# Rounding the attention heads to fp8 on VectorE: five bf16 operations in SBUF in place of four through a PSUM bank

## What is computed

```python
FP8_MAX = 448.0
def _fp8_roundtrip(x):
    return x.astype(jnp.float8_e4m3fn).astype(jnp.float32)

def _div_clamp_fp8(x, scale):
    y = jnp.clip(x.astype(jnp.float32) / scale, -FP8_MAX, FP8_MAX)
    y = y.astype(jnp.bfloat16).astype(jnp.float32)
    return _fp8_roundtrip(y)
...
core = _gqa(q, k, v).reshape(b, s, nh * d)
xout = _gqa(qx, kx, vx).reshape(b, s, nh * d)
cat = jnp.concatenate([core, xout], axis=-1)
catq = _div_clamp_fp8(cat, proj_smooth)
return jnp.einsum('bsi,oi->bso', catq, wproj) * (proj_in_scale * proj_w_scale)
```

## Time and profile before

| | us |
|---|---|
| median of 3 runs | 1740.62 (1740.0 to 1741.47) |
| the profiled execution | 1740.71 |
| its span | 1738.9 |
| PE busy | 1648.4 (95%) |
| DVE busy | 1411.2 (81%) |
| ACT busy | 1357.8 (78%) |
| POOL busy | 1085.3 (62%) |

### The profile page before, as it was taken

The page is one execution under the profiler, slowest core; times in us unless marked ns, Lnnn a source line. Parts: engine busy times, 40 slices in busy tenths (PEclk is TensorE's granted clock), DMA queues, the critical chain, the costliest instruction groups (busy, mean ns, idle before and its releaser), DMA issues.

```text
span 1738.9 us, 44071 instructions
## 1 busy us (share of the span) xinstructions
PE 1648.4 (95%) x15776; PEld 1228.6 (71%) x15776; DVE 1411.2 (81%) x3223; ACT 1357.8 (78%) x2907; POOL 1085.3 (62%) x1031
## 2 busy tenths in 40 slices
PE   1459999999999999999999999999999999999999
PEld 1438788888888888888888888888888544444444
DVE  8999899999999999999999999998779762323232
ACT  6879999999999999999999999999999622122221
POOL 1347787778777777777777777777777613121211
PEclk9879999999999999999999999999999999999999
DMA  5937788887878888888788888877999980303000
GB/s 177 214 95 133 142 157 146 146 154 148 144 149 154 153 147 152 144 148 148 150 145 151 148 158 149 144 142 132 175 203 196 201 244 26 134 12 140 6 24 25
DMA packets 663555, 241.45 MB, mean 139 GB/s; under 512 B 619440, under 2 KB 635952, under 8 KB 662832
## 3 DMA queue, kind: packets, MB, share of 16 engines
q1 hardware_dynamic: 662048, 230.20, 67.2%
q0 software_dynamic: 1296, 8.52, 2.4%
HBM read 75.15 MB, written 29.51 MB: 60 GB/s over the span
## 4 chain that ended last, share of the span: by engine, by line
PE 80%; ACT 6%; DVE 5%; issue 3%; SPq 2%; POOL 2%; DMA 1%; ACTq 0%; POOLq 0%; DVEq 0%
PE ps_pj L662 25%; PE ps_o L709 6%; PE ps_o L711 6%; PE ps_o L710 6%; PE ps_s L725 5%; PE ps_s L726 5%; PE ps_s L729 5%; PE ps_s L669 4%; PE ps_qt L681 4%; PE ps_pj L798 2%; PE ps_s L813 2%; PE ps_o L799 2%; PE ps_pj L799 2%; PE ps_o L798 2%; PE ps_s L812 2%
## 5 line engine op out<-in xcount | busy, mean ns | idle before, releaser
L1092 POOL TENSOR_TENSOR local<-local 128x512 bf16<-128x512 f32 x512 | 593.3, 1159 | 289.2 <-ACT local L998 288.9
L662 PE MATMUL ps_pj<-wide 128*128 128x256 bf16 (+1 forms) x5544 | 584.0, 254 | 5.3 <-DVE wide L1172 4.5
L662 PEld LDWEIGHTS ps_pj<-wide 128*128 128x128 bf16 x5544 | 469.9, 98 | 116.4 <-DVE wide L1172 4.7
L995 ACT ACTIVATE local<-ps_s,neg_max 128x512 f32<-128x512 f32 x512 | 389.2, 760 | 35.9 <-DVE neg_max L1359 33.8
L998 ACT ACTIVATE local<-ps_s,neg_max 128x512 bf16<-128x512 f32 x512 | 391.4, 764 | 0.0
L709 PE MATMUL ps_o<-v_hi,local 128*128 128x129 bf16 x2048 | 375.9, 222 | 2.8 <-DMA local<-local 1.4
L711 PE MATMUL ps_o<-v_hi,local 128*128 128x129 bf16 x2048 | 375.5, 219 | 0.0
L710 PE MATMUL ps_o<-local 128*128 128x128 bf16 x2048 | 375.3, 218 | 0.0
L1359 DVE TENSOR_REDUCE neg_max<-ps_s 128x1 f32<-128x512 f32 x512 | 345.2, 674 | 22.7 <-PE ps_s L729 22.1
L926 ACT ACTIVATE local<-ps_pj,head_rstd 128x128 f32<-128x128 f32 x756 | 239.6, 439 | 42.9 <-issue 41.2
L1069 POOL TENSOR_TENSOR head_rstd<-sq_sum,minus_half 128x3 f32<-128x3 f32 x256 | 226.2, 884 | 28.9 <-DVE sq_sum L1248 28.9
(11 more groups left out here) (126 smaller groups left out, 2622.6 us busy)
## 6 DMA issues: line engine op xcount, KB each, us to landing
quantised_heads<-local SPq DMA_DIRECT2D x128, 128.0 KB, 2.5
w_raw<-w_group SPq DMA_DIRECT2D x56, 256.0 KB, 3.1
wide<-quantised_heads SPq DMA_DIRECT2D x3, 4096.0 KB, 13.2
local<-local SPq DMA_TRANSPOSE x640, 3.2
wide<-packed_weights SPq DMA_DIRECT2D x32, 256.0 KB, 3.2
wide<-x SPq DMA_DIRECT2D x7, 1024.0 KB, 8.6
packed_weights<-w_proj POOLq DMA_DIRECT2D x4, 1024.0 KB, 15.3
wide<-quantised_heads SPq DMA_DIRECT2D x16, 256.0 KB, 3.3
```

The costliest lines, as they stand in the source:

```text
L662: last = mm(dst[:, at:at + n], lhs, w_at(par, part, c, cross * 512 + at, n), start=(k == 0), stop=(k == len(terms) - 1))
L995: a(p_exp[:, u % 2], ps_s[u % 2][:], ACT.Exp, bias=neg_max[:, u % 4:u % 4 + 1])
L1092: tt_(pp[:, u % PP_BUFS, 1], p_exp[:, u % 2], pp[:, u % PP_BUFS, 0], ALU.subtract)\
```

## The change

The bank `ps_y` is no longer used for the rounding. Its place is taken by `head_mag`, 512 bf16 in SBUF, in a stretch that was left empty. `y` is clipped to plus or minus 448 first, in place; the mask works on 512 int16; bounding from below and the multiplication by 24 are one operation in place; adding and subtracting are plain two-tensor operations. There is one more semaphore, between the clip and the mask.

```diff
-MAX_BINADE = 256.0
...
-        carve.at += T
+        head_mag = carve([T], BF16)
...
+        head_clipped = sem("head_clipped")
...
                         dve.wait_ge(total_done, GROUP_HEADS * g + H + 1)
                         if not first or H >= 2:
                             dve.wait_ge(turned[H % 2], 16 * GROUP_HEADS // 2 * g + 16 * (H // 2))
-                        v.scalar_tensor_tensor(heads_n[:, H % 2], ps_y[:], -KEEP4, summed, ALU.mult, ALU.add)\
+                        v.tensor_tensor(heads_n[:, H % 2], summed, head_mag, ALU.subtract)\
                             .then_inc(heads_done, 1)
...
                     for H in head_at(slot, QUANT_LAG, first):
                         dve.wait_ge(y_done, SLOTS * g + TT * (H + 1) + UNIT_FREE)
-                        v.tensor_scalar(ps_y[:, T // 2:T].bitcast(I32), y[:, H % 2].bitcast(I32), EXPONENT << 16 | EXPONENT, None,
+                        v.tensor_scalar(y[:, H % 2], y[:, H % 2], FP8_MAX, -FP8_MAX, ALU.min, ALU.max).then_inc(head_clipped, 1)
+                        dve.wait_ge(head_clipped, GROUP_HEADS * g + H + 1)
+                        v.tensor_scalar(head_mag.bitcast(I16), y[:, H % 2].bitcast(I16), EXPONENT, None,
                                         ALU.bitwise_and).then_inc(binade_done, 1)
                         dve.wait_ge(binade_done, GROUP_HEADS * g + H + 1)
-                        v.tensor_scalar(ps_y[:], ps_y[:, T // 2:T].bitcast(BF16), MIN_BINADE, MAX_BINADE, ALU.max, ALU.min).then_inc(mag_done, 1)
+                        v.tensor_scalar(head_mag, head_mag, MIN_BINADE, KEEP4, ALU.max, ALU.mult).then_inc(mag_done, 1)
                         dve.wait_ge(mag_done, GROUP_HEADS * g + H + 1)
-                        v.scalar_tensor_tensor(summed, ps_y[:], KEEP4, y[:, H % 2], ALU.mult, ALU.add).then_inc(total_done, 1)
+                        v.tensor_tensor(summed, y[:, H % 2], head_mag, ALU.add).then_inc(total_done, 1)
```

## The result

| | before | after |
|---|---|---|
| median of the runs beside each other (us) | 1740.31 | 1812.39 (1811.49 to 1813.22, 4 runs) |
| span of the profiled execution | 1738.9 | 1810.4 |
| from the first head's add to the last head's (start to start) | 1269.7 | 1340.4 |

The changed kernel is slower by 72 us: ratio 1.0413, 95% interval 1.0401 to 1.0425. The forecast was 1793, its range ended at 1807. The direction held and most of the mechanism; the size did not.

The account below looks back on a forecast made before the run. The prediction took TensorE to set the pace at 9.93 us a head, the other engines close behind. Sum: 1740.7 + 54 (123 heads, 0.44 us each) - 2 (drain) = 1793 us; range 1739 to 1807.

Parts of the forecast that it names:

- The work itself: VectorE's rounding operations alone, in SBUF instead of PSUM: shorter by 0.50 + 0.26 = 0.76 us a head.
- The neighbour, and the walk: Rounding beside GpSimd: clip held under L1092, add 0.01 behind L1076 and held, ending at 583.00, 1.13 us later.
- Rival (c): At the tie of add and L1076 the add is first; not slower, 1739.7 us, range 1738 to 1742; chance 0.20.
- Rival (b): At the same tie the add loses in about half of the heads: 1767 us; chance 0.14.
- What is late next, and one turn of 10.37: Maximum and exponential behind the add start late; the ScalarE/GpSimd/VectorE loop turns in 10.37 us against TensorE's 9.93.
- 123 x 0.44: Heads rounded before the drain, each 0.44 us longer by the loop: +54 us.
- (a): GpSimd first at the tie, add held: 1793 us, or 1807 with the subtract's 0.43 every fourth head; chance 0.60.
- ScalarE's 4.96 between two pairs: Part of the loop's turn: 4.96 us from the end of one exponential pair to that two units on.
- The last subtract: Rounding's final operation, two SBUF inputs, can be held by L1076 or L1092; priced at nothing, at worst 0.43 us.
- The drain, -2: Last five heads, where ScalarE waits for maxima: a rounding shorter by 0.50 gives back up to 2.5, taken as -2 us.

Follow-up runs that it names:

- experiments 6 and 7 without the clip: Changed kernel without its clip, L1172 (weights' low half) replaced by a row sum from the third group on: 1741.01 us; or asked for three slots later: 1741.48 us.
- experiment 3: Changed kernel with max/mult over 256 of a head's 512 columns only: 1759.58 us in one run.
- Experiment 6: Changed kernel, clip kept, with L1172 (low half of the weights) replaced by a row sum of the same length from the third group on: 1794.62 us.
- experiment 4: Kernel before, its four operations through PSUM kept, with two unused row sums of `y` behind them: 1824.97 us in one run.

## Why the prediction was wrong in its size

By its steps:

- *The work itself.* Right: AND and max/mult 0.29, the free add 0.42 (424 to 426 ns), the free subtract 0.41. None of the 0.76 gained in a head reached the end; even with both collisions gone (experiments 6 and 7 without the clip) the time is that of before, as TensorE bounds it.
- *The neighbour, and the walk.* Right to 0.02 us: clip 0.96, the add 0.01 behind L1076, its end 0.28 behind L1076's. The walk's order of starts decided, as it took it, in 117 heads. That it had the two in the right order was in part luck: its margin of 0.01 was as small as the rounding of the rows and smaller than what its estimates can carry, and it gave the other order a chance of 0.20 for that. (The add that comes first would have ended 582.06 - 581.87 = 0.19 later than now, not 0.18; nothing hangs on it.) Rival (c) said that the add would be first from 0.03 us on; 0.06 was enough (experiment 3), anything between was not tried. Rival (b), half of the heads, did not occur: the pattern repeats to 0.01 us, so a tie falls the same way each time.
- *What is late next, and one turn of 10.37.* Right where nothing else is in the turn: 10.38 in three heads of four, and the sum of that loop held for two other delays.
- *123 x 0.44.* This is the step that failed. It took one turn for all heads. One head in four carries the low half of a weights' chunk, and the prediction priced VectorE's 0.43 for the subtract in "every fourth head" as the upper end of (a), but not L1172. The term that is missing is 24 x (11.10 - 10.38) = 17 us: 24 powers are stretched in the steady part where none was before. Experiment 6, which takes the low half's second SBUF input away, measures it: 17.8. The walk looked only at operations that the change touches. It assumed that ScalarE's 4.96 between two pairs stays what it was when VectorE's other operations shift against GpSimd's, and one of them shifted from behind L1069 to the front of it.
- *The last subtract.* Priced at nothing, and it costs nothing: median 0.97 long after the change, 0.69 in the kernel without clip and low half, which is level with before (1.0005). In experiment 6's changed kernel it is 0.95 long, and all heads turn in 10.38, where the loop without it gives 10.36. The 14 us that the range held for it were for a cost that does not exist, and the real one, of nearly the same size, came on top of where it was looked for. The forecast plus 17 gives 1810.
- *The drain, -2.* Right: the last three intervals took 28.3 us for 30.5. Behind the last add nothing came back (+0.3).

What the two traces say in sum, cut at the starts of the adds: +0.6 ahead of the first, +1.5 over 8 intervals, +63.4 over the next 100 (44 and the 17 of the low half make 61), +7.9 over 16 (7.0 by 0.44 each), -2.2 over the last 3, +0.3 behind: the 71.5 us between the spans.

The Trainium skill, page "SBUF — State Buffer", section "Who interferes with whom", says that the issue order, not the shape, decides who blocks. By that rule the add should be free whenever it starts first; the starts of the experiments agree: held at 0.01 us behind, free at 0.06, 0.17 and more ahead, and then L1076 is longer in the first two, by 0.22 and 0.12 us. What the prediction took from the same section, that whoever is first has the ports for the whole instruction, fits these pairs but not GpSimd's power L1069: a VectorE operation that starts under it keeps its length (last section). The Trainium skill's page "VectorE: DVE Perf Modes", section "The perf-mode tier table", ranks bf16 in SBUF above any form with PSUM. The lone durations agree (0.29 against 0.70 of L1408), and the time went the other way.

## What to carry to other kernels

Before VectorE work is moved from PSUM into SBUF, lay it beside GpSimd's instructions start by start: forms with two SBUF inputs, and the fast one-input forms, were as long as the neighbour made them (L1092 and L1076 here, not the power), and the slower forms through PSUM kept their length. Then walk the full repeat of the pattern, here four heads, with every other operation of the queue in it, since a collision that is harmless by its order can turn round. Where two starts lie within a few hundredths, look for the 0.1 us that decides them: here a wait between two operations that did not need it was worth 57 us.

## What the runs showed of the hardware

- Two starts 0.01 us apart (8 to 14 ns) kept their order in all 117 heads in which the add and L1076 met so. A shift of 0.07 us turned it, and was worth 46 us where the work taken out makes 9.
- GpSimd's power on 3 columns, 0.85 us long, was held to 1.84 by a two-input VectorE operation of 1024 columns that had started 0.09 us earlier. A neighbour with almost no data of its own is blocked too. The other way round it blocked nothing: in the kernel before, the same VectorE operation started 0.37 behind the power's start, 0.48 before its end, in 24 cases and took its usual 1.21, and in the changed kernel the AND started 0.22 to 0.24 behind the power's start in 118 heads and took 0.29 to 0.30.
- A cast to bf16 of 1024 f32 columns takes 0.68 us when it is free (experiment 4) and 1.62 when it starts 0.09 behind a GpSimd L1092. In the kernel before, that hold is what puts L1172 behind L1069 by the starts: 0.9 us earlier it would be 0.5 in front. In the experiments that leave L1172 in its place, the cast is out of the hold and 24 powers are long. No run frees the cast alone, so that a hold can keep a kernel in order is argued from the starts and not shown.
- A row sum of 1024 f32 columns took 1.199 to 1.204 us in all 24 cases beside the same neighbours: this reduction with one input kept its length.
